# Attention in three of four layers: order of the scores, shift of the scores in four tiles of 32 rows, sums of weights in column tiles, rotation by shuffle

## The reference, as far as it matters

```python
# layer 0: 16 heads of 64, causal; the first 32 values of each head are rotated
t_rot = t_rot * cos + concat([-x2, x1]) * sin      # x1, x2: the two halves (16 each) of t_rot
scores = einsum('bhid,bhjd->bhij', q, k) * scale
out = softmax(scores) @ v
# layer 1: 8 heads of 32, keys and values from a latent of 64, all keys
# layer 2: 16 heads of 8, all keys
# layer 3: 16 heads of 64, biased projections, all keys, but the last key is masked for the first query
```

## Time and profile before

| | |
|---|---|
| three runs | 5903.27, 5914.32, 5922.73 us; median 5914.32 us |
| profiled execution | 5932.53 us, its span 5931.2 us, granted clock 0.906 |
| TensorE (PE) busy | 5068.7 us, 85% of the span |
| VectorE (DVE) busy | 3504.1 us, 59% |
| ScalarE (ACT) busy | 2389.9 us, 40% |
| GpSimd (POOL) busy | 1870.1 us, 32% |
| attention of layer 0 | 82.4 to 1235.2 us |
| attention of layer 1 | 2320.6 to 2992.5 us |
| attention of layer 2 | 3219.5 to 4140 us |
| attention of layer 3 | 4399.3 to 5871.8 us |

### The profile page before, as it was taken

How to read it: one execution, slowest core, us unless ns; L and a number is a source line. 1 busy time by engine, 2 the same in 40 slices (tenths; PEclk the granted TensorE clock), 3 DMA queues, 4 the chain that set the end, 5 groups by cost and what they waited for, 6 DMA issues and landing times. The chain is left out here.

```text
span 5931.2 us, 70306 instructions
## 1 busy us (share of the span) xinstructions
PE 5068.7 (85%) x28336; PEld 2586.9 (44%) x28336; DVE 3504.1 (59%) x4979; ACT 2389.9 (40%) x3274; POOL 1870.1 (32%) x904
## 2 busy tenths in 40 slices
PE   6999999967767676888867999999579999999997
PEld 3454545445544454333333222222345555555554
DVE  4666666545444545777733777774446666666664
ACT  2333333333333332545522666666124444444443
POOL 0444443521000110666710000000005555555563
PEclk9999999978778886988988999999779999999998
DMA  0000000000000000000000000000000000000000
GB/s 29 3 4 4 3 3 3 1 17 5 5 15 9 5 5 2 2 2 2 1 20 2 2 2 1 2 1 2 6 4 2 3 3 3 3 1 3 3 1 14
DMA packets 61718, 28.77 MB, mean 5 GB/s; under 512 B 38820, under 2 KB 57681, under 8 KB 61137
## 3 DMA queue, kind: packets, MB, share of 16 engines
q1 hardware_dynamic: 61392, 24.28, 1.6%
HBM read 23.21 MB, written 1.05 MB: 4 GB/s over the span
## 5 line engine op out<-in xcount | busy, mean ns | idle before, releaser
L785 DVE TENSOR_REDUCE L_part<-banks 128x2 f32<-128x1024 f32 (+2 forms) x1600 | 1882.6, 1190 | 836.9 <-PE banks L644 699.3
L770 ACT ACTIVATE L_weights<-banks 128x1024 f32<-128x1024 f32 (+1 forms) x1600 | 1580.2, 998 | 1544.0 <-PE banks L677 1264.5
L703 PE MATMUL banks<-L_weights,L_V 128*32 128x512 f32 (+3 forms) x6400 | 1516.4, 612 | 4.3 <-ACT L_weights L770 2.0
L968 POOL TENSOR_TENSOR L_wsum<-L_wsum,L_weights 128x1024 f32<-128x1024 f32 (+1 forms) x448 | 978.9, 2185 | 72.7 <-ACT L_weights L770 7.8
L951 POOL TENSOR_TENSOR L_wsum<-L_wsum,L_two 128x1024 f32<-128x1024 f32 x240 | 569.9, 2375 | 1218.0 <-DVE L_two L941 1217.3
L703 PEld LDWEIGHTS banks<-L_weights,L_V 128*64 128x64 f32 (+1 forms) x6400 | 286.3, 124 | 480.9 <-issue 423.4
L677 PE MATMUL banks<-L_QH,L_KH 64*128 64x512 f32 (+3 forms) x1664 | 388.2, 462 | 48.5 <-DVE SACC L836 32.0
L644 PE MATMUL banks<-L_KH,L_QH 64*128 64x512 f32 (+3 forms) x1664 | 350.5, 431 | 20.6 <-ACT L_weights L770 14.2
L941 DVE TENSOR_TENSOR L_two<-L_weights 128x1024 f32<-128x1024 f32 x240 | 338.9, 1412 | 39.0 <-ACT L_weights L770 38.5
L677 PEld LDWEIGHTS banks<-L_QH,L_KH 64*128 64x128 f32 x1664 | 158.4, 187 | 395.5 <-issue 225.9
L677 PE MATMUL banks<-L_QL,L_KH 64*128 64x512 f32 (+3 forms) x1664 | 325.7, 387 | 0.0
(11 more groups left out here) (460 smaller groups left out, 6505.5 us busy)
## 6 DMA issues: line engine op xcount, KB each, us to landing
F_tab<-xpos SPq DMA_DIRECT2D x8, 512.0 KB, 3.4
F_h<-L_ffn_h_w SPq DMA_DIRECT2D x2, 1024.0 KB, 7.5
F_wqkv<-L_ffn_wqkv SPq DMA_DIRECT2D x2, 768.0 KB
L_cos<-rope_cos SPq DMA_DIRECT2D x1, 1024.0 KB, 5.1
L_sin<-rope_sin SPq DMA_DIRECT2D x1, 1024.0 KB, 7.1
out<-X SPq DMA_DIRECT2D x1, 1024.0 KB, 5.1
F_w<-L_ffn_w_w SPq DMA_DIRECT2D x3, 256.0 KB, 3.6
F_w<-L_ffn_w SPq DMA_DIRECT2D x2, 341.0 KB
```

Of the source, the lines that this page charges most:

```text
L703: mm = pe.e.matmul(O[r, c:BANK], self.V[g % 2][:, kt, h, :], self.W[x % self.NW][:, y, c:BANK], start=kt < starts, stop=kt >= tiles - starts)
L770: act.e.activation(self.W[x % self.NW][:, :, c:BANK], self.banks(it)[:, :, c:BANK], ACT.Exp, scale=self.scale).then_inc(self.exped, 1)
L785: dve.e.tensor_reduce(self.part[n % 3][:, pr, j, p, :], self.banks(it)[:, :, 0:wide], AX.X, ALU.max).then_inc(self.mx_read, 1)
L968: pool.e.tensor_tensor(acc[:, :, c:BANK], acc[:, :, c:BANK], W[:, :, c:BANK], ALU.add).then_inc(self.summed, 1)
```

## The change

It has five parts.
1. In the pass without `APART` both scores stand next to each other, ahead of the pieces; the last pieces stand at the end of the pass, right ahead of the next pass's scores; in layers with `wide` heads (0 and 3) the last but one product goes between the two value steps. Layer 0 is no longer `APART`. Layer 2 stays so.
2. Layers 0 and 3: the shift is no longer a term of each score. `most` writes the maxima twice, 32 columns apart, so that QM has them in rows 0, 32, 64 and 96; ahead of the score of an even step four matmuls of 32 rows write the shift of both heads of both steps into the four banks, and the scores add three terms to it.
3. `den` in layers 0, 1 and 3: a stationary tile of ones of 128 by 32, four products into four column tiles, each over 256 of the weights' 1024 columns; VectorE transposes the result in blocks of 32 (DVE transpose) and takes the reciprocal of one column of each.
4. Layer 0: only the `straight` product is made. VectorE multiplies it by cos and by sin, shuffles the second result in blocks of 32 partitions (halves of 16 exchanged) and adds; the high half (ScalarE, new item `high`) stands at the start of the next pass, the low half behind it. The second weight tiles, their loads and memsets go.
5. Names: products no longer carry a head index.

Cut to its core:

```diff
     def plan(self):
-            items += early
+            items += early + [("high",) + it[1:] for it in carried]
             half = -(-len(ps) // 2)
-            if x + 2 < steps:
-                assert ("shift", self.step[x + 2][0]) in items, (x, self.step[x + 2])
-                items.append(("score", x + 2))
-            after = ([("score", x + 3)] if x + 2 < steps else []) + ps[half:]
+            scores = [("score", x + 2), ("score", x + 3)] if x + 2 < steps else []
+            assert not scores or ("shift", self.step[x + 2][0]) in items, (x, self.step[x + 2])
             if self.APART:
                 cut = len(ys) // 2
-                items += ps[:half] + carried + turns + eager(ys[:cut][:-1]) + [("values", x)] + mid + eager(ys[:cut][-1:])
-                carried = [] if self.EAGER else low(ys[:cut])
-                items += after + carried + eager(ys[cut:][:-1]) + [("values", x + 1)] + eager(ys[cut:][-1:])
-                carried = [] if self.EAGER else low(ys[cut:])
+                items += scores[:1] + ps[:half] + carried + turns + eager(ys[:cut][:-1]) + [("values", x)] + mid + eager(ys[:cut][-1:])
+                items += scores[1:] + ps[half:] + eager(ys[cut:][:-1]) + [("values", x + 1)] + eager(ys[cut:][-1:])
             else:
-                items += ps[:half] + carried + turns + eager(ys[:-1]) + [("values", x), ("values", x + 1)] + mid + eager(ys[-1:]) + after
-                carried = [] if self.EAGER else low(ys)
+                cut = len(ys) - 2 if self.wide else len(ys) - 1
+                items += scores + ps[:half] + carried + turns + eager(ys[:max(0, cut)]) + [("values", x)] + (eager(ys[max(0, cut):-1]) if self.wide else [])
+                items += [("values", x + 1)] + mid + eager(ys[-1:]) + ps[half:]
+            carried = [] if self.EAGER else low(ys)
...
     def score(self, pe, it):
         S = self.grab(pe, it)
+        shifted = self.shifted(pe, it)
...
     def most(self, dve, n):
-            last = dve.e.tensor_reduce(self.negmax[n % 2][:, :, r:r + 1], src, AX.X, ALU.max, negate=True)
+            for r in (self.row[h], self.row[h] + self.again) if self.again else (self.row[h],):
+                last = dve.e.tensor_reduce(self.negmax[n % 2][:, :, r:r + 1], src, AX.X, ALU.max, negate=True)
...
 class SummedAttention(Attention):
     def denominators(self, pe, it):
-        for j in range(4):
-            for h in range(2):
-                mm = pe.e.matmul(Y[:, 2 * j + h:2 * j + h + 1], self.wsum[n % 2][:, h, j * P:(j + 1) * P], self.core.ones[:, :], start=True, stop=True)
+        wsum = self.wsum[n % 2][:, :, :].rearrange("p h (j b r) -> p (h j) b r", j=4, b=4)
+        for b in range(4):
+            mm = pe.e.matmul(Y[32 * b:32 * b + 32, 0:256], self.ones32[:, :], wsum[:, :, b, :], start=True, stop=True)
         mm.then_inc(self.y_made, 1)
+
+    def invert(self, dve, it):
+        n = it[1]
+        dve.wait_ge(self.y_made, self.y[it] + 1)
+        dve.wait_ge(self.inverted, n)
+        dve.e.transpose(self.sums[:, :, :], self.ybanked(it)[:, 0:256]).then_inc(self.y_dve, 1)
+        self.yread(dve, self.y[it])
+        if n >= 2:
+            dve.wait_ge(self.merged, 8 * self.no["join", n - 2])
+        dve.e.reciprocal(self.rec[n % 2][:, :, :].rearrange("p h j -> p (h j)"), self.sums[:, :, 0]).then_inc(self.inverted, 1)
...
 class WideAttention(SummedAttention):
     row = [0, 64]
+    again = 32
     def terms(self, n, pr):
-        a, m = self.columns(n), n % 2 * BANK
-        return [(at, [(q[self.rows(h), :], k[self.rows(h), :]) for h in range(2)]) for at, q, k in (
-            (a, self.QH, KH), (a, self.QL, KH), (a, self.QH, KL), (m, self.QM, self.onesrow))]
+        a = self.columns(n)
+        return [(a, [(q[self.rows(h), :], k[self.rows(h), :]) for h in range(2)]) for q, k in ((self.QH, KH), (self.QL, KH), (self.QH, KL))]
+
+    def shifted(self, pe, it):
+        x = it[1]
+        if x % 2 == 0:
+            both = [self.banks(it), self.grab(pe, ("score", x + 1))]
+            m = self.half(x)[0] % 2 * BANK
+            for h in range(2):
+                for y in range(2):
+                    r, c = slice(64 * h + 32 * y, 64 * h + 32 * y + 32), self.half(x + y)[3]
+                    pe.e.matmul(both[y][:, h, c:BANK], self.onesrow[r, :], self.QM[r, m + c:m + BANK], start=True, stop=False)
+        return True
...
 class RotaryAttention(WideAttention):
-    PARTS = ("straight", "turned", "low")
-    APART = True
...
     def stage_dve(self, dve, it):
-        if it[0] == "straight":
-            if self.former[it]:
-                self.have(dve, self.former[it])
-            dve.e.tensor_tensor(st[:, :], Y, self.cosT[:, s], ALU.mult).then_inc(self.y_dve, 1)
-            return
+        if self.former[it]:
+            self.have(dve, self.former[it])
         dve.wait_ge(self.roped, self.no[it] - 1)
-        dve.e.tensor_tensor(self.turned[:, :], Y, self.sinT[:, s], ALU.mult).then_inc(self.y_dve, 1)
+        dve.e.tensor_tensor(st[:, :], Y, self.cosT[:, s], ALU.mult)
+        dve.e.tensor_tensor(self.turned[0][:, :], Y, self.sinT[:, s], ALU.mult).then_inc(self.y_dve, 1)
         self.yread(dve, self.y[it])
-        dve.e.tensor_tensor(st[:, :], st[:, :], self.turned[:, :], ALU.add).then_inc(self.roped, 1)
+        dve.e.stream_shuffle(self.turned[1][:, :], self.turned[0][:, :], [*range(16, 32), *range(16)]).then_inc(self.spun, 1)
+        dve.wait_ge(self.spun, self.no[it])
+        dve.e.tensor_tensor(st[:, :], st[:, :], self.turned[1][:, :], ALU.add).then_inc(self.roped, 1)
```

More of the change, by code:

```diff
@@ L283 @@
 class Attention:
-    PARTS = ("straight", "low")
     EAGER = False
+    again = 0
     APART = False
     NQ, NW = 4, 4
-    FREED = {"straight": "dve", "turned": "dve", "v": "act", "den": "dve", "shift": "act"}
+    FREED = {"straight": "dve", "v": "act", "den": "dve", "shift": "act"}
     def __init__(self, core, ctx, name, heads, hd, causal=False, last_key_mask=False, scale=1.0):
@@ L325, in sb @@
         return self.ctx.enter_context(self.nc.sbuf_tensor(self.name + "_" + n, s, d))
-    def project(self, g, which, b, h):
-        return [(part, which, g, h, b) for part in self.PARTS]
     def pieces(self, n):
@@ L354, in plan @@
         chunks, steps = len(self.chunk), len(self.step)
-        parts = self.PARTS[:-1]
-        products = lambda g, which, b: [(part, which, g, h, b) for h in self.products for part in parts]
-        low = lambda its: [("low",) + it[1:] for it in its if it[0] == parts[-1]]
+        products = lambda g, which, b: [("straight", which, g, b)]
+        low = lambda its: [("low",) + it[1:] for it in its if it[0] == "straight"]
         eager = lambda its: [x for it in its for x in [it] + (low([it]) if self.EAGER else [])]
-        whole = lambda g, which, b: [u for h in self.products for u in self.project(g, which, b, h)]
+        whole = lambda g, which, b: [(part, which, g, b) for part in ("straight", "high", "low")]
         items = self.items = [("fetch", 0), ("arrive", 0)] + whole(0, 1, self.chunk[0][1])
@@ L369, in plan @@
         units, shifts, carried = [], [], []
-        made = {(0, 0, b): [len(self.products), -9] for b in range(4)}
-        made[1, 0, self.chunk[0][1]] = made[1, 0, self.chunk[1][1]] = [len(self.products), -9]
+        made = {(0, 0, b): -9 for b in range(4)}
+        made[1, 0, self.chunk[0][1]] = made[1, 0, self.chunk[1][1]] = -9
         arrived = {0}
@@ L410, in plan @@
                     gm, chm = self.chunk[m][0:2]
-                    if any(made.get(key, [0])[0] < len(self.products) or made[key][1] >= x for key in ((1, gm, chm), (0, gm, it[4]))):
+                    if any(made.get(key, x) >= x for key in ((1, gm, chm), (0, gm, it[4]))):
                         break
@@ L511, in place @@
     def place(self, it):
-        part, which, g, h, b = it
+        part, which, g, b = it
         if which:
@@ L616, in product @@
     def product(self, pe, it):
-        part, which, g, h, b = it
-        w, src, K, rows = self.proj(g % 2, h, which)[part == "turned"]
+        part, which, g, b = it
+        w, src, K, rows = self.proj(g % 2, which)
         Y = self.take(pe, it)
@@ L634, in piece @@
         g, ch = self.chunk[n][0:2]
-        for h in self.products:
-            self.have(pe, (0, g, h, p))
-            self.have(pe, (1, g, h, ch))
+        self.have(pe, (0, g, p))
+        self.have(pe, (1, g, ch))
         banks = self.grab(pe, it)
@@ L667, in score @@
         self.yread(pe, self.y["shift", n])
-        for h in self.products:
-            self.have(pe, (0, g, h, kt // 4))
+        self.have(pe, (0, g, kt // 4))
         S = self.grab(pe, it)
+        shifted = self.shifted(pe, it)
         kk = slice(kt * P, (kt + 1) * P)
@@ L676, in score @@
             for y, (q, k) in enumerate(term):
-                mm = pe.e.matmul(S[:, y, c:BANK], k[:, kk] if k.shape[1] == T else k[:, :], q[:, a + c:a + BANK], start=t == 0, stop=t == len(terms) - 1 and not (on or cut))
```

(15 more changed lines are left out.)

88 lines of the change are left out of this document (41 added, 47 removed).

## The result

Before: 5913.4 us, median of four runs (5903.3 to 5922.7). After: **5962.9 us** (5959.2 to 5969.2). The ratio is 1.0085 with a 95% interval of 1.0066 to 1.0105: **slower, by 50 us**. The forecast was 5900 in a range of 5710 to 6040, with 0.45 for faster and 0.40 for slower; the time lies in the range and on the other side of the likeliest case.

What follows compares the result with a forecast made beforehand. TensorE's issue was taken to bound layers 0 and 3, a ring of waits layer 1. Layer terms -26, +51 and -36 gave -11 on the profiled 5932.5, 5903 after allowing for the median, stated as 5900; range 5710 to 6040 us.

Steps and rivals of the forecast that it cites:

- the price of the shift: Layers 0 and 3: a four-tile slot at 0.50 us replaces 0.46 per pair of key tiles; +10 us in layer 3.
- named 0.3 to 0.4 as the sign: Profile after: 0.3 to 0.4 us expected from the four shift matmuls to the first slot of the scores.
- The wait for two pairs at once: Behind joins the shift slot wants both pairs of banks; +0.5 x 23 = +12 us in layer 3, joins +45 in layer 0.
- The rival of a drain at each change of form: TensorE's array drains at each change of form: 0.16 more twice a pair, +133 us, 6035; chance 0.07.
- The sums: Sums of weights as column tiles: 1.25 us less for each of 80 chunks; -40, -20, -40 us in layers 0, 1, 3.
- The order in layers 0 and 3: Scores side by side: layer 0 slots -46 and +6, layer 3 exponential waits -48, against added waits behind projections and joins.
- the exponential's wait: Layer 3: first pieces no longer wait for the exponential just before; -0.24 us in some 200 passes, -48 us.
- stalls behind projections: Layer 0: pieces wait on VectorE's work behind projections; +43 us for queries and +34 for passes with two key projections.
- The order in layer 1: First pieces take the last piece's banks: +31 us over 96 passes with two pieces, +40 us behind projections.
- The sign of VectorE over 75%: Layer 1, profile after: VectorE busy over 75%, in a stage of 700 to 740 us.
- Rotation: Layer 0: 64 turned products of 1.06 us leave TensorE, -68 us; VectorE gains a shuffle taken at 0.7 us.
- rival 1: All three layers: the waits are covered, so the slot savings mostly show; 5670 to 5850 us, chance 0.28.

Runs made afterwards that it cites:

- e8b_both_pairs_at_once: Changed kernel with the shift again a fourth term of each score, plus the first score of a pair waiting for both pairs' banks; 5915.5 us, ratio 1.0009.

## Why the prediction was wrong

The sum came out in layer 1 (+51 for +51) and not in layer 3 (+28 for -36); that layer 0 came near (-36 for -26) is a balance of errors. Layer 3 by its terms, forecast and measured: sums -40 and -42; the order -18 and -5; the wait of the four tiles for both pairs +12 and +48; the form of the shift +10 and +34; rotation, which doesn't touch it, 0 and -7. For the whole kernel they are, with the waits that the new order brings counted to the order: sums -100 and -153, rotation -68 and -25, order +90 and +105, shift with its joins +67 and +125. The shift's price and the rotation's gain are off by 58 and 43 us the wrong way, and the sums hide 53 of it.

- **The step that failed is the price of the shift**: "(0.50 - 0.46) x 256 = +10", with joins "+0.5 x 23 = +12" in layer 3, +45 in layer 0. In the place of these 70 or so, the four tiles cost 125 us. The slot itself was well guessed (a pair 1.93 us; my terms gave 1.88). What I did not see is that the last piece, which the new order puts between the values and the four tiles, pays for the change as well: 0.43 to the four tiles instead of 0.33 to a score. The form costs 34 us in layer 3, half of it as 0.17 to 0.19 in each pass without a wait. From the four tiles to the first slot of the scores it is 0.44, where I had named 0.3 to 0.4 as the sign. I had taken a crossing as a cost of the new slot, where it is a cost of both neighbours.
- **The wait for two pairs at once** is the larger half, 78 us. I had it for joins alone, and at 0.5 us each. In layer 3 it does stand at the joins, and costs 48 us with the lower clock behind it. In layer 0 it is also met behind last pieces: the masks of pieces, which the next pair's shift often follows, take 72 us in all with the two pairs at once and 33 without, from start to next start; and the clock there goes from 0.96 to 0.91.
- The Trainium skill ("TensorEngine Tiling (Array Packing)", Key Properties) says that a change of the tiling mode drains the array. The trace agrees: weight loads start with their matmul on both sides of the four tiles (4808.29, 4808.73). The rival of a drain at each change of form had +133 us for that; measured are 47.
- **The sums**: forecast -100, measured -153. The block took 1.88 us in place of the 1.87 of the earlier trace rows and takes 0.57, 80 x 1.31 = 105 us (100 forecast); most of the other 48 is the clock, which is what 64 columns gave back as well (-35). I had read the block as TensorE at work.
- **The order in layers 0 and 3**: the exponential's wait is gone from plain passes as forecast (4.61 became 4.38 us without the four tiles), but projections took it back: a pass of layer 3 with one ahead of the last piece takes 6.12 us for 5.67, and the value step behind a product between two value steps takes 1.63, 14 times, where one alone takes 1.01. It came to -5 us in layer 3 where I had -18 before joins. In the changed kernel the sign came in part only: the weight loads of layer 3's pieces wait 48 us for exponentials, before 69. In layer 0 the order was to give 40, less 77 for stalls behind projections; it cost 8 to 15.
- **The order in layer 1**: +71 forecast, +85 measured, the cause confirmed by the run that restored the ring with the scores left in place. That the layer came out at +51 is two errors of 14 that cancel: the sums gave 34 there, not 20. The sign of VectorE over 75% did not come (472 of 669 us, 71%).
- **Rotation**: -68, with +77 of stalls behind projections in the new order; measured -25 in all with the old one. The shuffle takes 0.73 us (0.7 taken):

```profile
L1091 DVE STREAM_SHUFFLE L_turned<-L_turned 128x512 f32<-128x512 f32 x64 | 46.5, 727 | 0.0
```

The 0.6 estimated from the Trainium skill ("VectorE: DVE Perf Modes", Rules for kernel authors) was too low, since it scaled the page's figure with the number of elements alone; the measurement decides.

Times in the range of rival 1 (5670 to 5850) were reached, but only without the parts that cost: sums and rotation with the old order take 5733 us, 3.0% under the kernel before.

Open: why the addition behind the shuffle takes 0.82 us where the one behind two products took 1.19, what took half of the rotation's gain, and whether the order of layer 0 could be mended alone; none of these was tried.

## What to carry to other kernels

A form of matmul that saves slots has to be priced with both of its neighbours and with what it must own before it starts; work that needs two buffers at once waits for the later of them. When buffers go round in a ring, write down which item takes whose after a reordering, and how much work stands between: in layer 1 this, not the place of the scores, cost 85 us. And time each part of a bundle alone: here two parts (sums, rotation) gave 178 us, and two others (order, shift in four tiles) took 230 away.

## What the hardware showed beyond that

Sixteen matmuls of one column, 1.9 us of weight loading with hardly a column to stream, were followed by the lower clock in 18 of 30 blocks of layer 0, and there the slots behind them took 0.43 us for 0.23. Filling the same block with 64 columns, of which one is used, left its length nearly as it was (1.88 and 1.93 us) and made the kernel 35 us faster. "Busy" in the profile does not tell the two apart; the clock in a window of 4 us behind the block does.

An idle TensorE does it too. In layer 3, with the added wait of `e8b_both_pairs_at_once`, idle stretches of 2.25 us behind joins were followed by the lower clock 15 times; without it they last at most 1.2 us, and the layer's clock is 1.00.
